# Second attention: half of a per-head sum moved to GpSimd, two VectorE operations merged, one scatter moved by a step

## The reference, cut to what matters

```
qkvb = h @ W_qkvb.T                    # 16 heads x (64 q, 64 k, 64 v, 1 beta)
q = elu(q) + 1;  k = elu(k) + 1;  beta = sigmoid(beta)
q = q / sum(q);  k = k / sum(k)        # per head, over its 64 columns
W = W + (beta * (v - W @ k)) * k.T;  out = W @ q      # W is zero before the first token
attn_out = (out / sqrt(64)) @ W_o.T;   x = x + g * layer_norm(h + attn_out)
```

## Time and profile before

| what | value |
|---|---|
| runs shown | 486.09, 486.87, 489.3 us; median 486.87 |
| the profiled execution: time / span | 486.82 us / 485.1 us |
| mean granted TensorE clock | 0.946 of full speed |
| busy share of the span | PE 86%, DVE 75%, ACT 60%, POOL 53% |
| the chain that ended last, by engine | PE 54%, DVE 26%, POOL 3%, ACT 3% |
| stretch of the second attention | about 190 to 360 us |

### The profile page before, as it was taken

One profiled execution on the slowest core, in us unless ns is written; L12 is line 12 of the kernel. 1 busy time (PEld: TensorE's weight loads), 2 busy tenths in 40 slices (PEclk: granted clock), 3 DMA queues, 4 the chain that ended last, 5 costly groups with the idle time before them and its releaser, 6 DMA issues.

```text
span 485.1 us, 11398 instructions
## 1 busy us (share of the span) xinstructions
PE 418.7 (86%) x2670; PEld 323.6 (67%) x2670; DVE 362.5 (75%) x1189; ACT 291.2 (60%) x753; POOL 254.7 (53%) x340
## 2 busy tenths in 40 slices
PE   2979953199999996878999999999897979999995
PEld 2657752199999995345655665566555558888885
DVE  5859986046666666899999999999945537777764
ACT  2447641045555553668888888887555247777771
POOL 4013757125545556334556677666566019776662
PEclk9999965579999998899999999999898999999999
DMA  8901226778888751432113140000001321332226
GB/s 242 284 19 42 75 59 157 131 205 256 259 234 256 200 163 52 100 77 66 45 24 77 39 95 19 5 25 13 11 23 45 101 59 37 85 99 77 63 82 204
DMA packets 60802, 49.79 MB, mean 103 GB/s; under 512 B 18124, under 2 KB 49933, under 8 KB 60738
## 3 DMA queue, kind: packets, MB, share of 16 engines
q1 hardware_dynamic: 52338, 36.96, 29.6%
q0 software_dynamic: 5056, 8.48, 5.3%
q10 hardware_dynamic: 3344, 3.62, 2.8%
HBM read 37.25 MB, written 13.73 MB: 105 GB/s over the span
## 4 chain that ended last, share of the span: by engine, by line
PE 54%; DVE 26%; issue 9%; ACT 3%; POOL 3%; DMA 3%; SPq 1%; DVEq 0%; ACTq 0%; POOLq 0%
PE bank L1848 9%; PE bank L1827 9%; PE bank L1882 5%; PE bank L2008 4%; PE bank L1819 3%; DVE qk_sums L1441 3%; PE bank L1941 3%; DVE sums L1464 3%; POOL sorted_tokens L841 3%; PE bank L1981 3%; DVE big L1434 2%; DVE work L1478 2%; PE bank L1836 2%; PE bank L2006 2%; PE bank L1838 2%
## 5 line engine op out<-in xcount | busy, mean ns | idle before, releaser
L856 POOL DMA_INDIRECT results<-work x94 | 92.8, 988 | 78.6 <-DVE work L1389 56.1
L1882 PE MATMUL bank<-late,work 128*128 128x512 f32 x192 | 93.5, 616 | 2.6 <-ACT work L1031 2.4
L998 ACT ACTIVATE work<-bank,mcol 128x128 f32<-128x128 f32 x94 | 43.0, 458 | 43.6 <-PE bank L1819 43.1
L1882 PEld LDWEIGHTS bank<-late,work 128*128 128x128 f32 x192 | 34.1, 197 | 33.2 <-issue 29.7
L1827 PE MATMUL bank<-work,big 128*128 128x128 f32 x376 | 51.5, 281 | 0.0
L1848 PE MATMUL bank<-big,work 128*128 x376 | 50.5, 278 | 0.1
L1827 PEld LDWEIGHTS bank<-work,big 128*128 128x128 f32 x376 | 47.4, 198 | 0.0
L1848 PEld LDWEIGHTS bank<-big,work 128*128 128x128 f32 x376 | 46.6, 195 | 0.3 <-issue 0.3
L1375 DVE TENSOR_SCALAR work<-bank,b_columns 128x128 f32<-128x128 f32 x94 | 28.6, 346 | 24.1 <-PE bank L1827 24.1
L1007 ACT ACTIVATE work<-bank,b_columns 128x128 f32<-128x128 f32 x94 | 29.7, 364 | 27.4 <-PE bank L1827 27.3
L841 POOL DMA_INDIRECT sorted_tokens<-late,router_at x32 | 31.2, 976 | 20.2 <-issue 8.2
(11 more groups left out here) (264 smaller groups left out, 1080.5 us busy)
## 6 DMA issues: line engine op xcount, KB each, us to landing
big<-in_W SPq DMA_DIRECT2D x47, 256.0 KB, 3.3
work<-sorted_tokens SPq DMA_DIRECT2D x94, 65.0 KB, 2.0
big<-results SPq DMA_DIRECT2D x14, 256.0 KB, 3.1
big<-in_w SPq DMA_DIRECT2D x48, 56.0 KB
sorted_tokens<-zeros SPq DMA_DIRECT2D x26, 65.0 KB, 2.1
big<-in_w SPq DMA_DIRECT2D x48, 32.0 KB
results<-work POOLq DMA_INDIRECT x94, 2.9
xres<-in_x SPq DMA_DIRECT2D x4, 256.0 KB, 5.5
```

Source lines behind the costliest of these rows:

```text
L856: pool.indirect_dma_start(ys[l], bass.IndirectOffsetOnAxis(xg[b][:, D:D + 1].bitcast(I32), 0), yo[b], None, bounds_check=TOPK * T - 1, oob ...
L998: act.activation(xgT[b % 2], bank[:, ends[b % 2], 0:P], ACT.Identity, bias=scale_shift[0], scale=scale_shift[1]).then_inc(e_xTc, 1)
L1882: last = pe.matmul(bank[:, 2 * k + i, :], h3T[b], Wqkvb[:, k * HD + i * 512:k * HD + (i + 1) * 512], start=True, stop=True)
```

## The change

Four edits, all in the second attention:

- A new POOL stage `folded`, right behind `product` in the same step: it adds the two 32-column halves of each head's 64 products, giving 16 x 32 = 512 columns in the second half of the same buffer. `qk_reduced` on DVE then waits for it and sums 512 columns in place of 1024.
- `weighted` is one operation over 1024 columns (two PSUM banks) in place of two over 512.
- In DVE's list `moments5` and `scale3` move ahead of `qk_reduced`, so that `qk_reduced`, `coefficient` and `weighted` stand one behind the other.
- In POOL's list the lag of `send1(0)` becomes 9 in place of 10.

```
-        DS, TAILS = 9, 4 + NT // 4
+        DS, TAILS = 8, 4 + NT // 4
...
+            def folded(t, b, q):
+
+                pool.wait_ge(d_qk, 2 * t + 1)
+                halves = rf[b % 2][:, 0:HD].rearrange("p (h i d) -> p h i d", h=NH, i=2)
+                pool.tensor_tensor(rf[b % 2][:, HD:HD + HD // 2].rearrange("p (h d) -> p h d", h=NH),
+                                   halves[:, :, 0, :], halves[:, :, 1, :], ALU.add).then_inc(d_qk, 1)
...
-                (5, residual), (0, add_results), (10, send1(0)), (6, double1), (3, product), (8, send1(1))])
+                (5, residual), (0, add_results), (9, send1(0)), (6, double1), (3, product), (3, folded), (8, send1(1))])
...
             def qk_reduced(t, b, q):
-                dve.wait_ge(d_qk, t + 1)
-                dve.reduce_sum(sums[:, 0, :], rf[b % 2][:, 0:HD].rearrange("p (h d) -> p h d", h=NH), AX_X).then_inc(d_sum, 1)
+                dve.wait_ge(d_qk, 2 * t + 2)
+                dve.reduce_sum(sums[:, 0, :], rf[b % 2][:, HD:HD + HD // 2].rearrange("p (h d) -> p h d", h=NH),
+                               AX_X).then_inc(d_sum, 1)
...
-                for k in range(2):
-                    n = NH // 2
-                    dve.tensor_tensor(vc[:, k * 512:(k + 1) * 512].rearrange("p (h d) -> p h d", h=n),
-                                      bank[:, 4 + k, :].rearrange("p (h d) -> p h d", h=n),
-                                      sums[:, 5, k * n:(k + 1) * n].unsqueeze(2).to_broadcast([P, n, DH]),
-                                      ALU.mult).then_inc(d_sum, 1)
+                dve.tensor_tensor(vc.rearrange("p (h d) -> p h d", h=NH),
+                                  bank[:, 4:6, :].rearrange("p a (h d) -> p (a h) d", d=DH),
+                                  sums[:, 5, :].unsqueeze(2).to_broadcast([P, NH, DH]), ALU.mult).then_inc(d_sum, 1)
...
-                (3, sigmoid_inverse), (3, sigmoid), (3, qk_reduced), (5, moments5), (3, coefficient), (1, scale3),
+                (3, sigmoid_inverse), (3, sigmoid), (5, moments5), (1, scale3), (3, qk_reduced), (3, coefficient),
                 (3, weighted), (7, places[0]), (2, feature(0)), (5, norm5), (0, measure3), (6, picks[0]),
```

## The result

The changed kernel takes **502.57 us** (median of 4 runs, 501.06 to 505.98) against 487.76 for the kernel before (486.09 to 489.3, 4 runs beside it): 1.031 times as long, 95% interval 1.0265 to 1.0355. The forecast of 492.2 (its terms add up to 492.26) had the sign right and 10.4 us too little; the time lies above the range. The profiled execution took 503.75 us, with a span of 501.9 and a mean granted clock of 0.931 (485.1 and 0.946 before).

A forecast was written before the change was run, and what follows sets the result against it. VectorE was taken to set the pace, at 9.69 us a tile. From 486.82 us, less 1.3 (tiles 0 to 6), plus 7.74 (tiles 6 to 15), less 1.0 (tail), came 492.2 us, 1.1% slower; range 485.5 to 498.

The forecast's parts named there:

- What VectorE loses: VectorE, sum's start to next feature: 2.03 us in place of 2.93, 0.90 shorter; the rest of its round stays.
- What GpSimd gets: GpSimd gets the fold, one addition of 512 columns, taken at 1.28 us between ends of 1.09 and 2.37.
- the dear fold: Rival: short runs make the fold dearer in every round; 0.5 us more gives 500 us; chance 0.12.
- The step that failed: VectorE's moments and scale, moved ahead of the sum, were to cost nothing, covered by its wait for the fold.
- the term from the product's start to the sum's: GpSimd's product, gap, fold and VectorE's seeing it: 2.37 + 0.07 + 1.28 + 0.15 = 3.87 us.
- The price named for a lost cover: Without VectorE's wait for the fold, moments and scale would take back 0.36 us a tile.
- The loop that closes: VectorE and GpSimd work in turn: 9.31 or 9.54 us a tile, a pair 18.85 in place of 19.37.
- The moved sends: Four DMAs between even fold and odd product: rounds into tiles 7, 9, 11 take 11.67 us, 13 and 15 10.67.
- The first six tiles: Tiles 0 to 6, without sends: five rounds counted at 0.26 us less each, 1.3 us less.
- The rival on the clock: Rival: TensorE's clock falls in all five collisions, 8.5 us more, about 500 us; chance 0.07.
- The tail: Last product to transposes of the last weighted values, 8.12 us before: 1.0 less; what follows only shifts.
- another page's rule: GPSIMD Engine Reference: 2.6 cycles of 1.2 GHz per element for two-input operations, which belong on VectorE; fold columns 1.11 us.

The follow-up runs named there:

- experiment 1: The changed kernel with the lag of send1(0) back at 10: 505.09 us, ratio 1.0361 to the kernel before.
- experiment 3: The changed kernel with three small two-input VectorE operations made one-input reduces (parts left out) and send1(0) at lag 10: 492.38 us, ratio 1.0092.
- experiment 7: The changed kernel at lag 10, three small operations and the second router's picks made one-input reduces (parts left out): 486.67 us, ratio 0.9975.
- experiment 5: The kernel before with send1(0) at lag 9 and nothing else: 487.61 us, ratio 0.999.
- Experiment 2: The changed kernel, lag 9, with three small two-input VectorE operations made one-input reduces (parts left out): 500.07 us, ratio 1.0251.
- experiment 8: The changed kernel with the fold replaced by a GpSimd memset of 1024 columns, the sum reading constants: 493.23 us, ratio 1.0101.
- experiment 6: The kernel before with the values weighted in one VectorE operation and nothing else: 489.80 us, ratio 1.0012.
- experiment 9: The kernel before with the fold and the sum over 512 columns, and nothing else: 494.29 us, ratio 1.0102.
- experiment 4: The changed kernel without the fold, sum over 1024 columns, send1(0) at lag 10: 492.35 us, ratio 1.0113.
- experiment 10: The changed kernel, nothing left out, lag 10, held operations rewritten as reduces, both picks behind the sum: 486.46 us, ratio 0.9969 to the kernel before.

## Why the prediction was wrong, step by step

- *What VectorE loses*: right. From the sum's start to the next feature it is 2.06 us (291.90 to 293.96), forecast 2.03.
- *What GpSimd gets*: right. The fold takes 1.26 to 1.27 us, forecast 1.28, so the short runs cost nothing that shows and the dear fold falls as a rival.
- *The step that failed* is the one that cost the rest at nothing: "the moments and scale moved ahead lie in the time in which VectorE waits for the fold". In the changed kernel there is no such wait. L1458, and in odd tiles the picks, read two inputs from SBUF and last as long as GpSimd's fold does, and what follows them in the chain comes after the fold. In tiles 8 and 9 of the kernel before, no addition stood beside this chain: GpSimd's product ended before L1451 began, and behind it came two sends (282.04) in the one and 1.21 us of idle time, up to the residual at 292.57, in the other. The fold was put into just that place. So the term from the product's start to the sum's, 3.87, measured 4.55 in tile 8 and 4.69 in tile 9. The price named for a lost cover, 0.36 us, was for two operations; the whole of the chain behind L1458 comes to 0.85. How much the held operations are worth shows with the sends at lag 10: rewriting those of the chain brings 505.09 down to 492.38, and the picks as well 486.67 (experiments 1, 3 and 7).
- *The loop that closes*: its parts were right, the sum not. With the held operations rewritten, product to sum is 3.73 us (278.79 to 282.52) and a pair takes 19.23, against 18.85 forecast and 19.37 before. So even the cured loop gains little. That "the rest of the round stays as it is" doesn't hold: in tile 9 the two picks behind the sum cost 0.2 us, and from tile 8's sum to the next product VectorE needs 5.86 us in place of 5.44, as it idles for TensorE's router logits (L404 at 286.38) and for GpSimd's residual (L292 at 286.64; the residual ends at 286.50, behind fold and sends).
- *The moved sends*: right where the collision decides. Rounds into tiles 7, 9 and 11 took 11.59, 11.56 and 11.56 (forecast 11.67), into 13 and 15 10.61 and 10.62 (forecast 10.67). The rounds between took 10.16 to 10.43 where 9.54 was forecast; for those of 10.41 to 10.43 the failed term (4.69 less 3.87) is 0.82 of that. In the kernel before the same move costs nothing that the times can tell (experiment 5). That the forecast had the sign right is in part luck: it took the sends for the cause, and with the sends put back the kernel is as slow (experiment 1).
- *The first six tiles*: forecast 1.3 us less, measured 5.4 more. Experiment 2 takes 57.21 there with three operations rewritten. A part, 1.7 us, goes with TensorE's clock: the round from tile 1 to 2 took 11.43 us, with a granted clock of 0.89 on average between its two levels (1.2 and 2.4 GHz) from 212 to 224 us, after TensorE had waited 1.73 us for the weighted values at 207.94 to 209.67. Experiments 1, 5 and 8, with 0.81, 0.86 and 0.94 in that stretch, took 12.15, 11.43 and 11.44; the kernel before and all the others show 1.00 there and took 9.74 or 9.75. Experiment 5 has the same instructions as the kernel before up to there, so this part can't be put down to the change. Nor does the wait alone tell: experiment 2 waited 1.82 us at the same place and kept 1.00. Why the clock falls is open. The rival on the clock had such a loss in it, but in the collisions.
- *The tail*: forecast 1.0 less, measured 1.0 more from the last product on. The transposes of the last weighted values do come earlier, 6.82 us behind the product (362.70 to 369.52) where 8.12 was measured before, so "What follows the transposes only shifts" doesn't hold: from there to the end of the span it is 2.3 us more than before. No experiment shows why.

How the 3.1% come together: lag 9 and the one weighting cost nothing that can be told by themselves, the fold alone 1.0%, VectorE's order with the one weighting 1.1%, and all three 3.6% (experiments 5, 6, 9, 4, 1). The parts don't seem to add, though the intervals leave little room to say so. The order puts two more operations into the chain that the fold holds up: the sum starts 0.4 to 0.6 us later in experiment 1 than in 9.

The trace before held a sign of it, which the prediction passed over. The scale took 0.33 us in one tile and 0.54 in the next. GpSimd's and VectorE's timelines of the kernel before:

```profile
274.28 0.46 POOL L885 TENSOR_TENSOR xres<-xres,big 128x128 f32<-128x128 f32 x1
...
274.28 0.54 DVE L307 TENSOR_SCALAR ln_xn<-xres,ln_mv,ln_r 128x128 f32<-128x128 f32 x1
```

The longer one, of tile 7, ends at 274.82, just behind GpSimd's addition at 274.74.

The Trainium skill, SBUF — State Buffer, section Who interferes with whom, says that a VectorE instruction with two SBUF inputs contends with a GpSimd instruction that reads SBUF and not with one that only writes, that whichever comes first keeps the shared ports to its end, and that tensor_reduce doesn't contend. The runs agree on what contends and what doesn't: 1.17 us beside the fold, 0.18 beside the memset, 0.19 for the reduce beside the fold. On who comes first they show GpSimd's side plainly, and of VectorE's only a hint: in experiment 2 the residual's last addition (L892 at 300.27) took 0.52 us, against 0.45 to 0.46 elsewhere, where the scale had begun at 300.13. The prediction had weighed another page's rule and not this one.

## What to carry to other kernels

Before work is given to GpSimd, list what VectorE does in that stretch and mark every operation that reads two inputs from SBUF: here each lasted until GpSimd's addition had ended, and the rest of a chain of small ones then started where the wait was meant to end. A product or a sum of rows that lie side by side can be written as one reduce, which wasn't held; here that, with two picks moved behind the sum, brought 505 us back to 486, the time of the kernel before. And a duration far above its like can be a wait, though the profile counts it as busy time.

## What the runs showed of the hardware beyond that

- The scale (L307, one tensor of 128 columns and two numbers per partition, from SBUF to SBUF) is held too: 0.65 us in experiment 10, ending at 282.57 just behind the fold, against 0.33 beside a send. So a tensor_scalar can be held where a reduce (0.19 to 0.21) and a reciprocal (0.25) beside the same fold are not.
- A VectorE operation with one input in PSUM and one in SBUF wasn't held: L1441 took 1.22 us at 293.96 to 295.18 in the changed kernel, beside the residual's and the results' additions on GpSimd, as it does elsewhere, and these took their usual 0.46.
- The holder need not be long: one_hot in the last kernel took 0.40 us at 292.74, beside one of GpSimd's operations of 0.45 us (292.60 to 293.05), where it took 0.22 beside the memset.
